# Moving the loading of the weights of a four-layer graph network into its sort phase

## The reference

```python
h = relu_layernorm(x)
x = x + L0(h)   # softmax-weighted sum of relu(h[src]) per node, then relu(. @ W1 + b1) @ W2 + b2
x = x + L1(h)   # relu(batchnorm([h[row], h[col]] @ W1 + b1)), the same with W2, summed per node
x = x + L2(h)   # two spline convolutions over 27 weight matrices, elu
x = x + L3(h)   # three rounds of relu(h[src] + e), summed per node, @ W + b, leaky relu
```

## Time and profile before

| | |
|---|---|
| median of 3 runs | 7850.94 us (7818.64, 7850.94, 7851.61) |
| profiled execution | 7858.02 us |
| its span | 7856.2 us, 39070 instructions |
| TensorE matmul busy | 2708.5 us (34%) |
| VectorE busy | 4300.7 us (55%) |
| ScalarE busy | 1275.8 us (16%) |
| GpSimd busy | 5213.5 us (66%) |
| mean granted TensorE clock | 0.691 of full |

### The profile page before, as it was taken

One profiled execution on the slowest core, in us unless ns is written; L12 is line 12 of the kernel. 1 busy time (PEld: TensorE's weight loads), 2 busy tenths in 40 slices (PEclk: granted clock), 3 DMA queues, 4 the chain that ended last, 5 costly groups with the idle time before them and its releaser, 6 DMA issues. The chain is left out here.

```text
span 7856.2 us, 39070 instructions
## 1 busy us (share of the span) xinstructions
PE 2708.5 (34%) x8375; PEld 1703.4 (22%) x8375; DVE 4300.7 (55%) x7258; ACT 1275.8 (16%) x2189; POOL 5213.5 (66%) x5106
## 2 busy tenths in 40 slices
PE   0000000005323300287745552776233365365222
PEld 0000000003211100133323332554133133233111
DVE  6999979921244700255548887778666422322311
ACT  0000000001111200276621010111244011011000
POOL 4777778887777277775567772663477476476477
PEclk9999999966555655698867776777555555555555
DMA  1111110013333000112212221221344222222111
GB/s 45 24 31 27 26 23 19 18 21 104 98 51 49 13 23 23 30 43 53 47 40 42 42 41 46 33 33 23 79 78 75 56 39 37 57 40 35 59 35 30
DMA packets 364618, 331.80 MB, mean 42 GB/s; under 512 B 115499, under 2 KB 339968, under 8 KB 363379
## 3 DMA queue, kind: packets, MB, share of 16 engines
q0 software_dynamic: 163072, 77.69, 11.5%
q1 hardware_dynamic: 199282, 249.37, 9.6%
q10 hardware_dynamic: 2048, 2.41, 0.1%
HBM read 173.11 MB, written 158.67 MB: 42 GB/s over the span
## 5 line engine op out<-in xcount | busy, mean ns | idle before, releaser
L889 POOL DMA_INDIRECT c_ring<-tab,QB x784 | 762.6, 973 | 614.5 <-POOLq L102 298.9
L889 POOL DMA_INDIRECT g_ring<-tab,QB x784 | 743.3, 948 | 420.4 <-issue 238.4
L889 POOL DMA_INDIRECT l_ring<-in_x_dram,a_own x392 | 538.4, 1373 | 130.9 <-issue 119.2
L1338 POOL DMA_INDIRECT nodes<-l1s_rowr,a_out x392 | 386.2, 985 | 264.3 <-DVE l1s_rowr L1354 145.1
L2007 POOL DMA_INDIRECT out_dram<-out_rowr,out_idxr x392 | 386.4, 986 | 221.9 <-issue 123.3
L1461 PE MATMUL c_psU<-spline,c_hzT 96*128 96x288 f32 x1568 | 516.8, 477 | 40.5 <-DVE c_V L1425 40.2
L889 POOL DMA_INDIRECT sort_ring<-in_x_dram,sort_raw x392 | 412.7, 1053 | 120.5 <-issue 119.2
L889 POOL DMA_INDIRECT l_ring<-agg_tab,QA x392 | 401.7, 1025 | 135.3 <-issue 119.2
L889 POOL DMA_INDIRECT H<-xe_tab,idx_a x392 | 406.0, 1036 | 122.6 <-issue 118.9
L889 POOL DMA_INDIRECT rows_b<-b_edges,idx_b x392 | 399.4, 1019 | 130.5 <-issue 118.9
L889 POOL DMA_INDIRECT c_ring<-nodes,b_other x392 | 386.9, 987 | 128.7 <-issue 118.0
(11 more groups left out here) (480 smaller groups left out, 8291.5 us busy)
## 6 DMA issues: line engine op xcount, KB each, us to landing
tab<-M SPq DMA_DIRECT2D x5, 6272.0 KB
nodes<-l_xout SPq DMA_DIRECT2D x40, 322.3 KB
nodes_x<-nodes SPq DMA_DIRECT2D x50, 257.8 KB
c_din<-dst_lin SPq DMA_DIRECT2D x98, 128.0 KB, 2.8
c_ring<-tab,QB POOLq DMA_INDIRECT x784, 3.3
dst_lin<-c_yd SPq DMA_DIRECT2D x98, 128.0 KB
g_din<-dst_lin SPq DMA_DIRECT2D x98, 128.0 KB, 2.8
g_ring<-tab,QB POOLq DMA_INDIRECT x784
```

The lines of the kernel that those rows point to most:

```text
L889: pool.indirect_dma_start(out=ring[:, at + j, :], out_offset=None, in_=table, in_offset=bass.IndirectOffsetOnAxis(ap=idx[:, w:w + 1], axis ...
L1338: pool.indirect_dma_start(out=g.nodes2, out_offset=bass.IndirectOffsetOnAxis(ap=A.out[:, w:w + 1], axis=0), in_=rowr[k % NR][:, j, :], in_ ...
```

## The change

The phase `load_weights` becomes a class `Weights` whose parts are called from the blocks of the sort phase. Its tiles and semaphores now belong to that phase. The list of loads is the same one. The parts:
- `clear` on VectorE, after the clearing of `space` and before `net.top`: the memsets of all weight tiles, of the constants and of `mean`, then `cleared`.
- `identity` on GpSimd, behind the memsets of `raw` and `key` and ahead of the iotas.
- `load` on ScalarE, behind the two copies of the attributes and ahead of the wait for `decoded`: the DMAs of the list, issued by ScalarE's queue in place of SyncE's.
- `finish` on VectorE, behind `ranked` and ahead of the segment flags: `mean`'s diagonal, `center`, `avg`, the wait for the loads, `rb1`, and `alone`.
- `tensor` on TensorE, behind `join.tensor`; the latter now starts with a wait for the identity.

The core of the diff, with the list of the loads left out:

```diff
+    def load(self, act):
+        act.wait_ge(self.cleared, 1)
+        for dst, src in self.loads:
+            with self.g.nc.allow_non_contiguous_dma(reason="columns and small blocks of weights"):
+                act.dma_start(dst, src).then_inc(self.loaded, 16)
+
+    def identity(self, pool):
+        g = self.g
+        pool.memset(g.ident[:, :], 0.0).then_inc(self.blank, 1)
+        pool.wait_ge(self.blank, 1)
+        pool.affine_select(out=g.ident[:, :], in_=g.ident[:, :], pattern=[[1, P]], compare_op=ALU.not_equal,
+                           fill=1.0, base=0, channel_multiplier=-1).then_inc(self.made, 1)
+
+    def clear(self, v):
+        g, link = self.g, Link(v, self.filled)
+        for t in (g.w0a, g.w0b, g.w1s, g.w1d, g.w2, *g.root, *g.w3, *g.we):
+            link.inc(v.memset(t[:, :], 0.0))
+        link.inc(v.memset(g.ones[:, :], 1.0))
+        link.inc(v.memset(g.eps[:, :], 1e-5))
+        link.inc(v.memset(g.zeros[:, :], 0.0))
+        link(v.memset(g.mean[:, :], 0.0))
+        v.sem_inc(self.cleared, 1)
+        return link
+
+    def finish(self, v, link):
+        g = self.g
+        for t in range(4):
+            link.inc(v.memset(g.mean[t * D:(t + 1) * D, t * D:(t + 1) * D], 1.0 / D))
+        v.wait_ge(self.filled, link.n)
+        v.wait_ge(self.made, 1)
+        link.inc(v.tensor_tensor(g.center[:, :], g.ident[:, :], g.mean[:, :], ALU.subtract))
+        link(v.tensor_tensor(g.avg[:, 0:2 * D], g.ident[:, 0:2 * D], g.ident[:, 2 * D:4 * D], ALU.add))
+        link(v.tensor_tensor(g.avg[:, 0:D], g.avg[:, 0:D], g.avg[:, D:2 * D], ALU.add))
+        link(v.tensor_scalar(g.avg[:, 0:D], g.avg[:, 0:D], 0.25, None, ALU.mult))
+        for t in range(1, 4):
+            link.inc(v.tensor_copy(g.avg[:, t * D:(t + 1) * D], g.avg[:, 0:D]))
+        v.wait_ge(self.loaded, 16 * len(self.loads))
+        link(v.tensor_scalar(self.rb1[:, :], g.b0col[0:2 * D, :], 0.0, None, ALU.max))
+        v.tensor_copy(self.rb1w[:, :], self.rb1[:, 0:1].broadcast_to([2 * D, P])).then_inc(self.mlp0, 1)
+        v.wait_ge(self.mlp1, 1)
+        link(v.tensor_copy(g.alone[:, :], self.psc[:, 0:D]))
...
@@ order_edges
+        weights = Weights(ph, g, a)
...
             pool.memset(key[:, :, :], FAKE).then_inc(padded, 1)
+            weights.identity(pool)
             pool.iota(slot[:, :], [[1, SF]], base=0, channel_multiplier=SF).then_inc(made, 1)
...
         def _(pe):
+            pe.wait_ge(weights.made, 1)
             join.tensor(pe)
+            weights.tensor(pe)
...
             act.copy(table[:, :, 4:12], raw8).then_inc(rows_made, 1)
+            weights.load(act)
             act.wait_ge(decoded, 1)
...
             v.memset(space[:, 0:11 * W], 0.0).then_inc(blank, 1)
+            filled = weights.clear(v)
             net.top(v, link)
...
             v.sem_inc(ranked, 1)
+            weights.finish(v, filled)
             v.wait_ge(back, 16 * 4)
...
@@ build
-            load_weights(g, a)
```

More of the change, by code:

```diff
@@ L122, in block, with __init__ @@
         return self.ctx.enter_context(self.nc.Block())
[L125 to L135, removed]
+class Weights:
+    def __init__(self, ph, g, a):
+        self.g = g
+        self.made, self.loaded, self.cleared = ph.sem("w_made"), ph.sem("w_loaded"), ph.sem("w_cleared")
+        self.blank, self.mlp0, self.mlp1, self.filled = (ph.sem("w_" + n) for n in ("blank", "mlp0", "mlp1", "filled"))
+        self.psc = ph.ps("w_psc")
+        self.rb1, self.rb1w = ph.sb("w_rb1", [2 * D, 1]), ph.sb("w_rb1w", [2 * D, P])
+        self.w2c = w2c = ph.sb("w_w2c", [2 * D, D])
+        self.loads = loads = []
         def diagonal(dst, src, rows, cols, times):
@@ L223, with tensor @@
+    def tensor(self, pe):
+        g = self.g
+        pe.wait_ge(self.mlp0, 1)
+        pe.matmul(self.psc[:, 0:D], self.rb1w[:, :], self.w2c[:, :], start=True, stop=False)
+        pe.matmul(self.psc[:, 0:D], g.ones[0:1, :], g.bias[:, 0, :], start=False, stop=True).then_inc(self.mlp1, 1)
 SR, SF = 98, 512
```

## The result

| | us |
|---|---|
| kernel before, median of 4 | 7838.82 (7818.64 to 7851.61) |
| changed kernel, median of 4 | 7769.94 (7760.51 to 7779.99) |
| ratio, 95% interval | 0.9908 (0.9889 to 0.9926) |
| profiled execution, its span | 7779.99, 7778.2 |

The account below looks back on a forecast made before the run. The prediction took the first 73 us as serial load issue and the sort phase as GpSimd-bound: 7858.02 - 72.97 + 0.8 = 7785.9 us profiled, 7779 us against the median, range 7742 to 7810 us.

Parts of the forecast that it names:

- The front that goes: Start of the kernel: without the old loading phase and its barrier, GpSimd's sort work begins 72.97 us earlier.
- Identity: GpSimd, before the iotas: 0.74 us of work fits into the 1.31 us wait for `dst`, so 0 us.
- Clear: VectorE, sort start: 3.0 us of memsets, 0.8 given back, 2.2 us later under 21.4 us of cover at `joined`; costs 0.
- Finish: VectorE, end of sort phase: 3.9 us more work, within 33.5 us of waiting; slightly slower gathers cost 0.8 us.
- The loads on ScalarE: ScalarE's queue, sort phase: 154 loads take 63 us (52 to 154), inside 298 us before `decoded` is met; 0 us.
- The loads beside the gathers: GpSimd's first gather series: some 50 gathers run beside the loads; price from 0 to 47 us, taken as 0.
- The rival that had 47 us here: First gather series: gathers slowed beside the loads, 1.88 instead of 0.95 us each, giving 7826 us; chance 0.08.
- ScalarE's queue as the bound: Rival, sort phase: loads of over 3.3 us each delay the sorted indices and second series; 7937 us at 4.3; chance 0.03.
- TensorE's clock: Rival, later phases: granted clock falls differently from 0.75; 7817 us at 0.73, 7877 at 0.70; chance 0.05.
- The later phases: Behind the sort phase: each starts at an all-engine barrier, moves rigidly with that phase's end and lasts the same to a few us.

Follow-up runs that it names:

- The kept phase: Against the changed kernel, the first phase stays with clearing, identity, mean, centre and average; only the loads and what needs them move to the sort phase: 7770.47 us.

## Why the prediction was right

- **The front that goes**, 72.97 us: right. The memset of `raw` is at 0.75 us, the first gather 77.35 - 4.45 = 72.9 us earlier, the second series 73.6, L0 73.7. The kept phase shows 6 of them to be VectorE's work and its barrier.
- **Identity**, 0 us: right. The wait for `dst` behind it shrank from 1.31 to 0.77 us, and the first gather came at 4.45 us (4.4 forecast).
- **Clear**, 3.0 us, hidden: 5.38 to 8.38 us, 3.0 us. The 0.8 us given back at the program's start did not come: VectorE started at 1.72 us, 0.97 behind GpSimd, not at 0.88. The store issued at `joined` is 17.6 us ahead of the second series and not 21.4: 3.9 us less, where 2.2 us were forecast. Neither mattered.
- **Finish**, 3.9 us and 0.8 us to pay: it took 3.7 us (894.35 to 898.05). VectorE's waits at the end fell from 33.5 to 26.2 us (27 forecast). The 0.8 us cannot be seen: the second series lasted 405.8 us, 406.0 before.
- **The loads on ScalarE**, 0 us: right. They were issued from 19.04 to 87.46 us, 0.44 us each (0.41 forecast, from 22 to 90 us). They started beside ScalarE's two copies, which ran from 19.04 to 22.92 us, and not behind them: here the issue of a DMA did not wait for the copy ahead of it to end. On the slower chips they took 0.90 to 1.27 us each, which goes beyond the upper bound of 1.00; they were through by 215 us, still far ahead of the index store (553.6 us or later).
- **The loads beside the gathers**, 0 us: right, and it has a direct control. The same 80 us of the series in both kernels (columns as in the earlier trace rows), before without loads:

```profile
93.00:173.00 80.00, 0.00 (x0) 0.00 (x0) 77.68 (x120) 2.56 (x1) 61.41 (x62) 1.00 0.19 56
```

and after, with all but the first few of the loads in it:

```profile
20.00:100.00 80.00, 0.00 (x0) 0.00 (x0) 77.71 (x119) 2.92 (x2) 61.38 (x62) 1.00 0.26 62
```

62 gathers took 61.41 and 61.38 us, while the DMA engines' share rose from 0.19 to 0.26. The rival that had 47 us here falls; no price at all is seen.
- **ScalarE's queue as the bound**: the mechanism is real (551.8 us of waiting with 1554 loads), its condition was far off: 0.44 us each against the 3.3 us from which it decides.
- **TensorE's clock**: 0.689 over the span against 0.691, and again 0.75 in the stretch of the earlier trace rows, 84 us earlier, with 1374 us of matmul:

```profile
3116.00:5516.00 2400.00, 1374.24 (x4277) 852.61 (x4278) 1655.32 (x2491) 680.32 (x1103) 1414.70 (x1428) 0.75 0.21 42
```

So this rival did not come. That it exists shows in the kernel with L0's work broken up, where one phase got 0.89 for 0.85 and was 21 us shorter. What follows L0 lasted 5782.6 us before, 5788.6 after and 5774.5 in the second profile of the changed kernel, so it scatters by 14 us between executions.
- **The later phases** are what the prediction had wrong: each was to move rigidly with the end of the sort phase and last the same to a few us. L0 lasted 7 to 15 us less than before in the four profiles with its code unchanged (910.0 to 917.3 against 924.7), for the most part since the gathers stood otherwise against VectorE's runs. That, less the 6.0 us behind L0, made the span's gain 78.0 where the steps give 73.7. The steps themselves were added up to 72.2 us, and the start of L0 shows 73.7. That the medians give 68.9 and 72.2 us (7835.58 less 7763.4) and come so near the 72 forecast is in part luck, since what lies outside the steps scatters by more than 10 us.

## What to carry to other kernels

A serial prologue of small DMAs is issue time here (0.41 to 0.44 us each on the first chip, up to 1.27 on the others); it was free on a queue behind which nothing is due for as long as it lasts, and cost 33 us on one that a ring of buffers depends on. So ask of a moved step who is queued behind it, before asking what it costs. Where GpSimd's indirect DMAs are the limit, look in the timeline for single gathers as long as a two-input VectorE instruction or a run of them; waiting for each instruction on VectorE may slow it and still shorten the phase.

## What the runs showed of the hardware

- A gather, 0.95 us beside a one-input reciprocal of 19.75 us, lasted 26.55 us beside a run of 32 `scalar_tensor_tensor` and 12.88 us beside one product of 13.20 us. With a wait behind each instruction none lasted over 5 us.
- The kernel before took 7836, 9407 and 9440 us on three chips. On the slower ones VectorE's instructions last the same (a two-input operation on 98x512 0.69 us), but it has gaps in front of them that the profile puts down to its own last instruction, to nothing ("issue") or to "remote". ScalarE's queue issues more slowly too, 0.90 to 1.27 us for each of the 154 loads. Of the kernel with the 3.4 us operations broken up, VectorE's waits in the sort phase

```profile
DVE sort_x L255 <- DVE sort_x L256: 103.9, 91, 1.5
DVE sort_x L255 <- issue: 102.9, 64, 2.7
DVE sort_x L255 <- remote: 89.9, 40, 3.4
```

and of the changed kernel on the first chip, where the largest that is not a barrier or data is

```profile
DVE sort_x L290 <- issue: 0.5, 3, 0.2
```

The cause is not known. It moved the bound of the sort phase from GpSimd to VectorE, so a cover read on one chip does not hold on every other.
